# A graph layer, linear attention and a mixture of experts on one core: where the pass over the groups gets the graph branch's residual from

## The reference, cut to what matters

```
xn = _layernorm(x)
graph = relu(layernorm(gat_layer(xn, edges) + xn) * ln_gamma + ln_beta)
h     = xn + linear_attention(rmsnorm(xn))
mix   = h + rmsnorm(h, w_norm2)
x = x + graph + mix
x = x + moe(layernorm(x))          # top 2 of 8 experts
```

## Time and profile before

| | |
|---|---|
| median of 3 runs | 3586.68 us (3580.91 to 3588.13) |
| the profiled execution's own time | 3580.47 us |
| its span | 3578.8 us |
| mean granted TensorE clock | 0.901 |
| PE busy | 2793.4 us (78%) |
| DVE busy | 2344.6 us (66%) |
| POOL busy | 2154.1 us (60%) |
| ACT busy | 1288.4 us (36%) |
| HBM | 394.80 MB read, 132.72 MB written |

### The profile page before, as it was taken

One profiled execution on the slowest core, in us unless ns is written; L12 is line 12 of the kernel. 1 busy time (PEld: TensorE's weight loads), 2 busy tenths in 40 slices (PEclk: granted clock), 3 DMA queues, 4 the chain that ended last, 5 costly groups with the idle time before them and its releaser, 6 DMA issues. The chain is left out here.

```text
span 3578.8 us, 70224 instructions
## 1 busy us (share of the span) xinstructions
PE 2793.4 (78%) x17326; PEld 2290.8 (64%) x17327; DVE 2344.6 (66%) x6486; ACT 1288.4 (36%) x4257; POOL 2154.1 (60%) x2117
## 2 busy tenths in 40 slices
PE   6757788888888888888888888433335799999997
PEld 4535666666666666666666666323335799999997
DVE  6655666666566667777777777888878455555554
ACT  5723333333333333333333333355542233333332
POOL 3167777777776777776666666246656344444443
PEclk9979999999999999999999999755555899999999
DMA  7656666666665667666666666445582344444443
GB/s 246 238 133 155 159 159 155 160 158 161 158 157 147 155 158 191 184 184 179 179 175 176 171 170 169 134 153 175 182 277 101 74 71 71 71 71 71 71 71 52
DMA packets 384652, 529.69 MB, mean 148 GB/s; under 512 B 64276, under 2 KB 323559, under 8 KB 384218
## 3 DMA queue, kind: packets, MB, share of 16 engines
q0 software_dynamic: 114496, 265.49, 32.3%
q1 hardware_dynamic: 185112, 183.84, 18.2%
q10 hardware_dynamic: 84770, 77.19, 6.8%
HBM read 394.80 MB, written 132.72 MB: 147 GB/s over the span
## 5 line engine op out<-in xcount | busy, mean ns | idle before, releaser
L1119 POOL DMA_INDIRECT rows<-node_rows,index x1552 | 1475.7, 951 | 581.3 <-issue 446.5
L1397 PE MATMUL ps_sum<-msg,hot 128*128 128x260 f32 x3904 | 1021.7, 407 | 18.0 <-DVE big L1216 1.7
L1397 PEld LDWEIGHTS ps_sum<-msg,hot 128*128 128x128 f32 x3904 | 730.7, 197 | 134.2 <-issue 5.2
L2126 POOL DMA_INDIRECT out_dram<-big x204 | 353.3, 1732 | 437.8 <-DVE big L2218 388.7
L1199 DVE TENSOR_TENSOR msg<-rows,ps_w 128x1024 f32<-128x1024 f32 x488 | 596.2, 1222 | 16.9 <-issue 2.6
L1377 PE MATMUL ps_hot<-ident_h,hotT 128*128 128x128 bf16 x1952 | 194.5, 223 | 300.7 <-DVE hotT L1175 298.7
L2177 ACT ACTIVATE x_actT<-x_ps_hT,b1T 128x128 f32<-128x128 f32 x816 | 233.2, 369 | 523.0 <-PE x_ps_hT L2152 522.9
L1284 ACT ACTIVATE e<-e 128x16 f32<-128x16 f32 x488 | 105.3, 216 | 878.1 <-DVE e L1193 865.1
L2152 PEld LDWEIGHTS x_ps_hT<-x_rowsT,x_w_now 128*128 128x128 f32 x3264 | 398.1, 192 | 11.5 <-DVE x_w_now L2196 1.1
L1686 POOL DMA_INDIRECT expert_in<-f_rows,f_slot x196 | 260.4, 1329 | 231.6 <-ACT f_rows L1729 174.6
L2152 PE MATMUL x_ps_hT<-x_rowsT,x_w_now 128*128 128x128 f32 x3264 | 399.1, 276 | 0.7 <-DVE x_w_now L2196 0.7
(11 more groups left out here) (289 smaller groups left out, 4163.2 us busy)
## 6 DMA issues: line engine op xcount, KB each, us to landing
targets<-dst_row SPq DMA_DIRECT2D x391, 128.0 KB
big<-expert_in SPq DMA_DIRECT2D x204, 130.0 KB, 2.1
rows<-node_rows,index POOLq DMA_INDIRECT x1564
node_rows<-big SPq DMA_DIRECT2D x14, 924.0 KB
turned<-rT SPq DMA_DIRECT2D x14, 896.0 KB, 4.5
area<-turned ACTq DMA_DIRECT2D x98, 128.0 KB
queries<-area ACTq DMA_DIRECT2D x98, 128.0 KB
area<-queries ACTq DMA_DIRECT2D x98, 128.0 KB
```

The lines of the kernel that those rows point to most:

```text
L1119: g.indirect_dma_start(rows[:, j, k, :], None, s.node_rows, bass.IndirectOffsetOnAxis(ap=index[:, b, j * G + k:j * G + k + 1], axis=0)).th ...
L1397: mm = pe.matmul(ps_sum[:, j % 2, 0:SUM], hot[:, j % MSGS, k * P:(k + 1) * P], msg[:, j % MSGS, k, :], start=(k == 0), stop=(k == G - 1))
L2126: g.indirect_dma_start(out, bass.IndirectOffsetOnAxis(ap=rows[:, j, D:D + 1].bitcast(I32), axis=0), outs[:, j, :], None, compute_op=ALU.ad ...
```

## The change

The edge stage no longer stores xn, and the table `residual` is gone. `normalise` no longer waits for such a store. In the pass ScalarE makes xn from x (`renorm`), with the same scale and bias, in seven operations a group. It does so for group n + 1 in iteration n, behind `scale_tiles(n)` and ahead of `ffn_roots(n - 1)`; group 0 comes first of all. `renorm(c)` waits for x of group c and until `join(c - 2)` no longer reads the buffer. SyncE's `load(c)` now issues x first and mixed second. VectorE's L1821 waits for `renorm` where it waited for the loads, and `join` waits for mixed.

```diff
-    s.residual = nc.dram_tensor("residual", [NP, D], F32).ap()
@@ edge stage, ScalarE
                 def normalise(t):
                     act.wait_ge(x_in_done[u], 16 * (t // 2 + 1))
                     if t >= 2:
-                        act.wait_ge(xn_stored[u], 16 * (t // 2))
                         act.wait_ge(hh_ready, t - 1)
-                def store_xn(t):
-                    act.wait_ge(xn_ready, t + 1)
-                    act.dma_start(s.residual[t * P:(t + 1) * P, :], xn[:, t % 2, :]).then_inc(xn_stored[t % 2], 16)
@@ the pass, SyncE
                 def load(c):
                     if c >= 2:
-                        sp.wait_ge(summed, c - 1)
                         sp.wait_ge(joined, c - 1)
-                    for table, into in ((s.residual, xn), (s.mixed, hh)):
-                        sp.dma_start(into[:, u, :, :], table[...]).then_inc(loaded[u], 16)
                     sp.dma_start(x_row[:, u, 0:full, :], x[...]).then_inc(loaded[u], 16)
                     if c == CHUNKS - 1:
                         sp.dma_start(x_row[0:TAIL, u, CHUNK - 1, :], x[N - TAIL:N, :]).then_inc(last_loaded, 16)
+                    sp.dma_start(hh[:, u, :, :], s.mixed[...]).then_inc(mixed_in[u], 16)
@@ the pass, ScalarE
+                def renorm(c):
+                    u = c % 2
+                    if c >= 2:
+                        act.wait_ge(gain_used, 2 * (c - 1))
+                    act.wait_ge(loaded[u], 16 * (c // 2 + 1))
+                    if c == CHUNKS - 1:
+                        act.wait_ge(last_loaded, 16)
+                    for i in range(CHUNK):
+                        t = c * CHUNK + i
+                        act.activation(xn[:, u, i, :], x_row[:, u, i, :], ACT.Identity, bias=s.ln_bias[:, t:t + 1], scale=s.ln_scale[:, t:t + 1]).then_inc(renormed, 1)
+                def renorm_next(c):
+                    if c + 1 < CHUNKS:
+                        renorm(c + 1)
+                renorm(0)
                 act.wait_ge(mix_root_in, 1)
-                in_turn([gat_root, scale_tiles, ffn_roots, odds_of, make_rows], [0, 0, 1, 2, 1], CHUNKS)
+                in_turn([gat_root, scale_tiles, renorm_next, ffn_roots, odds_of, make_rows], [0, 0, 0, 1, 2, 1], CHUNKS)
@@ the pass, VectorE: divide
-                    v.wait_ge(loaded[c % 2], 48 * (c // 2 + 1))
+                    v.wait_ge(renormed, (c + 1) * CHUNK)
@@ the pass, VectorE: join
-                    then(v.tensor_tensor(gain[:, u, :, :], hh[:, u, :, :], gain[:, u, :, :], ALU.mult))
+                    v.wait_ge(mixed_in[u], 16 * (c // 2 + 1))
+                    v.tensor_tensor(gain[:, u, :, :], hh[:, u, :, :], gain[:, u, :, :], ALU.mult).then_inc(gain_used, 1)
...
+                    v.wait_ge(gain_used, 2 * c + 1)
+                    v.tensor_tensor(hh[:, u, :, :], gain[:, u, :, :], x_row[:, u, :, :], ALU.add).then_inc(gain_used, 1)
```

More of the change, by code:

```diff
@@ L1037, in attend_edges @@
         xn_ready = sem("m_xn_ready")
-        xn_stored = [sem(f"m_xn_stored{u}") for u in range(2)]
         attended = sem("m_attended")
@@ L1360, in _ @@
                          [(KV_AT, -3, load_rT), (KV_AT, 1, exponents), (KV_AT, 3, store_q),
-                          (MIX_AT, -3, load_mix), (MIX_AT, 0, normalise), (MIX_AT, 2, store_xn), (MIX_AT, 3, copy_headsT),
+                          (MIX_AT, -3, load_mix), (MIX_AT, 0, normalise), (MIX_AT, 3, copy_headsT),
                           (MIX_AT, 6, store_hh)])
@@ L1364, in _ @@
                 for u in range(2):
-                    act.wait_ge(xn_stored[u], 16 * (TILES // 2))
                     act.wait_ge(mixed_stored[u], 16 * (TILES // 2))
@@ L1542, in finish @@
         last_loaded = sem("f_last_loaded")
+        mixed_in = [sem(f"f_mixed_in{u}") for u in range(2)]
+        renormed = sem("f_renormed")
+        gain_used = sem("f_gain_used")
         stored = sem("f_stored")
@@ L1603, in load @@
                     if c >= 2:
-                        sp.wait_ge(summed, c - 1)
                         sp.wait_ge(joined, c - 1)
-                    for table, into in ((s.residual, xn), (s.mixed, hh)):
-                        sp.dma_start(into[:, u, :, :], table[c * CHUNK * P:(c + 1) * CHUNK * P, :].rearrange("(t p) d -> p t d", p=P))\
-                          .then_inc(loaded[u], 16)
                     sp.dma_start(x_row[:, u, 0:full, :], x[c * CHUNK * P:(c * CHUNK + full) * P, :].rearrange("(t p) d -> p t d", p=P))\
@@ L1612, in load @@
                         sp.dma_start(x_row[0:TAIL, u, CHUNK - 1, :], x[N - TAIL:N, :]).then_inc(last_loaded, 16)
+                    sp.dma_start(hh[:, u, :, :], s.mixed[c * CHUNK * P:(c + 1) * CHUNK * P, :].rearrange("(t p) d -> p t d", p=P)).then_inc(mixed_in[u], 16)
                 def store(c):
@@ L1843, in join @@
                     settle()
-                    if c == CHUNKS - 1:
-                        v.wait_ge(last_loaded, 16)
-                    then(v.tensor_tensor(hh[:, u, :, :], gain[:, u, :, :], x_row[:, u, :, :], ALU.add))
+                    v.wait_ge(gain_used, 2 * c + 1)
+                    v.tensor_tensor(hh[:, u, :, :], gain[:, u, :, :], x_row[:, u, :, :], ALU.add).then_inc(gain_used, 1)
                     then(v.tensor_tensor(tiles(c), tiles(c), to_tiles(lnbeta_b), ALU.add))
                     settle()
+                    v.wait_ge(gain_used, 2 * c + 2)
                     v.scalar_tensor_tensor(tiles(c), tiles(c), 0.0, hh[:, u, :, :], ALU.max, ALU.add).then_inc(joined, 1)
```

## The result

The changed kernel takes 3637.88 us (median of 4 runs, 3632.90 to 3644.83), the kernel before 3587.40 us (median of 4 runs, 3580.91 to 3589.74). The ratio is 1.0145, with a 95% interval of 1.0132 to 1.0158: 50.5 us slower. The profiled execution took 3640.41 us.

What follows compares the result with a forecast made beforehand. VectorE's order, with its waits, was taken to set the pass's pace. +52 for 12 intervals, +3.4 for the first group and -3 for the edge stage made +53 on 3580.5, 3633.5; predicted median 3639, range 3617 to 3657.

Steps and rivals of the forecast that it cites:

- The late root: In the pass, VectorE's L1866 gets ScalarE's first root at J + 12.7 instead of J + 6.8, 5.9 us late.
- J: In the pass, the moment a group's join ends, from which later moments are counted; 2505.62 in the group read.
- The 12 intervals: In the pass, between ends of joins: 32.5, 35.4 and ten of 36.4, together 432 against 379.7, +52 us.
- The load waits: VectorE's 36.5 us at L1821 in the pass: removal saves 0.15 to 0.9 us a usual group, some 14 for groups 2 to 13.
- The first group: Start of the pass: `scale_tiles(0)` and its 14 steps stand ahead of `renorm(1)`, +3.4 us at the first J.
- The edge stage: Second part of the edge stage: 98 removed stores lie beside other work; 3 us taken off.
- (1): Rival, in the pass: x's load does not queue behind the store; +12 in all, 3599; chance 0.06.
- (2): Rival, in the pass: x lands before J + 3.8 and `renorm` fills ScalarE's idle time; -14, 3573; chance 0.05.
- L: In the pass, x's landing counted from J: 9.0 us, and 8.0 in the first two intervals.
- (3): Rival, edge stage: all 21.5 us of gathered-row waits and some of ScalarE's 33 saved; +31, 3618; chance 0.07.
- (4): Rival, in the pass: scatters or weights hold x back another 1.5 us an interval; +71, 3657; chance 0.05.
- The estimate from the Trainium skill: In the pass, x lands behind the store at 6.2 us, making the 12 intervals 34 us shorter, +19 in all.

Runs made afterwards that it cites:

- The store kept: Changed kernel, with the edge stage storing xn again and the wait on it: 4510.00 us beside 4457.99, ratio 1.0123; repeated 4566.91 beside 4495.92, 1.0126.
- group 1 early: Changed kernel with x's load issued at the join's read, plus `renorm(1)` moved ahead of `scale_tiles(0)`: 3575.30 us beside 3583.42 of the kernel before, ratio 0.9978.
- x before the store: Changed kernel, with SyncE issuing x of group c + 2 ahead of group c's store: 4484.20 us beside 4457.99, ratio 1.0068; repeated 4529.95 beside 4495.92.

## Why the prediction was right

The forecast was 3639 us in a range of 3617 to 3657, slower with a chance of 0.93; measured 3637.88.

- *The late root.* Forecast: J + 12.7, VectorE waiting 65 to 70 us in all. Measured: J + 12.15 in the group shown, 68.5 us in 12 waits. The mechanism was the one forecast, wait by wait. The terms behind it, in that group: x at J + 9.0 (measured 8.5), 3.45 us of work (3.45), 3.2 us to L1881 (3.1), 10.2 to the group's root (10.2), 10.3 to the next join (10.3). The interval of 36.4 was 35.9. Most of the 0.5 us is the landing of x, which over the usual groups was 8.7 and not 9.0; before the scatters begin it was 7.9, for a forecast of 8.0.
- *The 12 intervals.* Forecast +52, measured 428.6 - 379.7 = +48.9. The usual interval of the kernel before was 31.3 rather than 31.2. The last interval of the changed kernel was 37.1: x of group 13 came 1.1 us later than usual (a root wait of 6.56 instead of 5.4), most likely because the weights had not quite drained, for which the forecast added nothing.
- *The load waits were not to be had.* L1841 waits 1.9 us in a usual group for ScalarE's root behind `make_rows` (22.3 us in all, where it was 5.1), as the one group of the earlier trace rows had shown.
- *The first group.* Forecast +3.4, measured 42.1 - 38.2 = +3.9. One sign of the forecast did not come: the add was to wait for nothing, and L1829 waited 8.9 us in the first two groups.
- *The edge stage.* Forecast -3, and no run shows it. In the profiled execution the stage ended at 2288.3 instead of 2281.8. Of these 6.5 us, 5.0 were there before the first of the removed stores: ScalarE's last operation of the keys and values' tiles began at 1270.4, not 1265.4, in code that is the same. From there to the stage's end it took 1017.9 us, where it had taken 1016.4. In the medians the time outside the pass is 2.3 us shorter on this chip and no shorter on another (see "The store kept"), less than runs of one kernel differ.
- *Luck.* The pass was forecast 55.7 us longer and was 52.8. That the whole came out within 2 us of the measured 50.5 owes something to the 3 us taken off for the edge stage, which made up for the 3 too many in the pass.
- *The rivals.* (1) x does not queue behind the store: fell, x lands at J + 8.5 and not at 5.6, and 2.5 us earlier once it is ahead of the store. (2) Faster, if x lands before J + 3.8: x lands later. The versions fit the condition as far as they go: with x at J + 8.7 and 6.0 the interval follows L + 27.4 to 0.2 us (35.9 and 33.3), and with x at J + 1.4 it is 31.0, below the 31.3 of the kernel before. No version put x near 3.8. (3) A large gain in the edge stage: fell, as above. (4) x held back still longer: not seen, apart from the last group.
- *The estimate from the Trainium skill.* By its page "DMA: Bandwidth & Descriptors", section "Anatomy of one DMA", whose fit is for transfers issued from GpSimd, x would land behind the store at 6.2 us, an estimate for two transfers on end. The trace has 8.5 to 9.0 with the store ahead and 6.0 without it, on SyncE's queue with scatters beside it. The measurement decides; the row of the trace was the nearer one by far.

## What to carry to other kernels

Work moved to an idle engine is free only if its input is there when its turn comes, and if it ends before another engine asks for what stands behind it. The same seven operations cost nothing in one place (they ended 2.1 us before the root was asked for), and 2 us a group behind the roots, without any wait, because `make_rows` had no such room. On ScalarE, which runs its program in order, one wait a group delayed everything queued behind it, and cost 82 us without any work. So ask who waits for what stands behind the new work, and make its input arrive earlier. Ask of each load what its buffer really waits for: here it was a read in the middle of the join, not the end of it, and 4 us and one place in a queue made the difference between a pass 53 us longer and one 3 us shorter. Price a change by the moment at which its first input lands, counted from the step that issues it; that one number was worth more here than all busy times.

## What was not expected of the hardware

On two of the chips the edge stage of the same program ran 850 to 880 us (the first) and 910 to 940 us (the second) longer, while the pass took the same time to within 1 us (565.1 us on the usual chip, 565.1 and 565.7 on the other two, for the same pass). Here is the stretch from 400 to 2000 us, in which both run the same code, in the version with group 1 early on the usual chip, and in the one with x before the store on the other: window, length, busy PE, PEld, DVE, ACT, POOL, clock, DMA share, GB/s.

```profile
400.00:2000.00 1600.00, 1347.39 (x8294) 1022.97 (x8292) 1065.95 (x2855) 552.97 (x1985) 1158.09 (x1219) 0.97 0.61 161
```

```profile
400.00:2000.00 1600.00, 1059.35 (x5674) 791.76 (x5673) 711.00 (x1857) 387.99 (x1399) 827.81 (x870) 0.83 0.42 111
```

Every engine does 65 to 71% of the instructions in that time. The granted clock is lower too, 0.83 for 0.97, and a matmul takes 187 ns for 162; but TensorE also stands still for 541 of the 1600 us instead of 253, so the clock is not the whole of it. TensorE's and GpSimd's waits in the first:

```profile
PE ps_hot L1369 <- DVE hotT L1173: 225.1, 192, 4.0
POOL rows L1117 <- SPq L1086: 88.5, 106, 4.0
```

and in the second, with gaps in which TensorE waited for nothing that the profile shows:

```profile
PE ps_hot L1369 <- DVE hotT L1173: 241.5, 54, 12.7
PE ps_hot L1369 <- issue: 111.6, 59, 7.4
POOL rows L1117 <- SPq L1086: 517.4, 116, 11.7
```

The waits are few and long there. GpSimd, which gathers the node rows, waits 517.4 us for what SyncE issues, instead of 88.5. No experiment was made on this, and the cause stays open. What it taught is to compare the stage that was changed by its own length, and whole times only beside the kernel before on the same chip.
